# Self attention: TensorE issues the scores of heads 2 and 3 after the weighted sums instead of before them

## What is computed

```python
q, k, v = split(x @ w_qkv.T)                       # 8 batches, 16 heads, 512 tokens, 16 channels
scores = einsum('bhqd,bhkd->bhqk', q, k) * scale + bias(table)
attn = softmax(scores, axis=-1)
out = einsum('bhqk,bhkd->bhqd', attn, v).reshape(B, N, C) @ w_proj.T + b_proj
x = layernorm(x + out)
```

## Time and profile before

| | us |
|---|---|
| three timed runs | 1013.95, 1016.24, 1019.85 |
| their median | 1016.24 |
| the profiled execution | 1011.83 |
| its span, first to last instruction | 1010.0 |
| TensorE busy (weight loads 512.2) | 922.5 |
| ACT busy | 745.1 |
| DVE busy | 701.5 |
| GpSimd busy | 295.2 |

### The profile page before, as it was taken

The page is one execution under the profiler, slowest core; times in us unless marked ns, Lnnn a source line. Parts: engine busy times, 40 slices in busy tenths (PEclk is TensorE's granted clock), DMA queues, the critical chain, the costliest instruction groups (busy, mean ns, idle before and its releaser), DMA issues. The chain is left out here.

```text
span 1010.0 us, 17742 instructions
## 1 busy us (share of the span) xinstructions
PE 922.5 (91%) x5301; PEld 512.2 (51%) x5301; DVE 701.5 (69%) x1838; ACT 745.1 (74%) x1414; POOL 295.2 (29%) x349
## 2 busy tenths in 40 slices
PE   5699999999999999999999999996089999999992
PEld 2234444444444433334333433433089989998991
DVE  5378777887878878355676675586257887887883
ACT  1478878787878778899999999983047767766761
POOL 4042313141313111001122212314413434434443
PEclk9699999999999999999999999997589999999996
DMA  8987689969696867878877697641353533543550
GB/s 224 238 216 204 151 226 246 244 183 222 193 221 181 211 164 167 178 182 180 169 159 127 134 186 144 123 93 42 103 200 126 211 133 128 184 174 133 174 207 31
DMA packets 74845, 172.04 MB, mean 170 GB/s; under 512 B 16658, under 2 KB 36040, under 8 KB 64713
## 3 DMA queue, kind: packets, MB, share of 16 engines
q1 hardware_dynamic: 67944, 156.36, 61.7%
q0 software_dynamic: 6496, 14.16, 4.0%
q10 hardware_dynamic: 320, 0.52, 0.2%
HBM read 122.23 MB, written 53.73 MB: 174 GB/s over the span
## 5 line engine op out<-in xcount | busy, mean ns | idle before, releaser
L780 ACT ACTIVATE probs<-sc 128x512 f32<-128x512 f32 x1024 | 530.3, 609 | 107.7 <-DVE sc L873 81.4
L510 PE MATMUL sc<-qst,kst 57*128 57x512 f32 (+1 forms) x1024 | 258.6, 468 | 11.8 <-DMA qst<-s_qk 9.7
L873 DVE TENSOR_TENSOR sc<-sc,strip 128x308 f32<-128x308 f32 (+1 forms) x512 | 192.3, 430 | 94.2 <-PE sc L510 93.0
L522 PE MATMUL ot<-probs,vals 128*32 128x512 f32 x1600 | 214.0, 607 | 0.2 <-issue 0.2
L510 PEld LDWEIGHTS sc<-qst,kst 57*128 57x128 f32 (+1 forms) x1024 | 117.4, 185 | 162.8 <-ACT probs L780 118.6
L1757 ACT ACTIVATE f_h<-f_h_ps,par 128x384 f32<-128x384 f32 x104 | 60.9, 586 | 31.9 <-PE f_h_ps L1667 31.9
L1834 DVE TENSOR_TENSOR f_h_lo<-f_h,f_h_hi 128x384 fp32r<-128x384 f32 x104 | 65.2, 627 | 13.7 <-DVE f_h_hi L1832 5.7
L1915 POOL DMA_INDIRECT home<-s_x,get_ids x45 | 51.6, 1146 | 76.1 <-issue 43.1
L879 DVE STREAM_TRANSPOSE turned<-ot 128x512 f32<-128x512 f32 x50 | 35.4, 708 | 49.4 <-PE ot L522 45.1
L1832 DVE CAST f_h_hi<-f_h 128x384 fp32r<-128x384 f32 x104 | 37.1, 356 | 41.5 <-ACT f_h L1757 41.3
L1928 POOL DMA_INDIRECT out<-f_normed,f_put_ids x39 | 43.0, 1103 | 64.6 <-ACT f_normed L1791 56.2
(11 more groups left out here) (189 smaller groups left out, 1615.3 us busy)
## 6 DMA issues: line engine op xcount, KB each, us to landing
s_qk<-w_hi SPq DMA_DIRECT2D x32, 512.0 KB, 7.4
strip<-in_w_all SPq DMA_DIRECT2D x16, 1024.0 KB, 7.8
f_raw<-in_w_all SPq DMA_DIRECT2D x14, 1024.0 KB, 6.5
s_x<-x SPq DMA_DIRECT2D x8, 1026.0 KB, 12.1
kst<-s_qk SPq DMA_DIRECT2D x32, 256.0 KB, 6.2
qst<-s_qk SPq DMA_DIRECT2D x32, 256.0 KB, 7.4
s_x_parts<-split SPq DMA_DIRECT2D x16, 512.0 KB, 3.1
kst<-s_ctx_parts SPq DMA_DIRECT2D x32, 256.0 KB, 6.3
```

The lines of the kernel that those rows point to most:

```text
L510: nc.tensor.matmul(sc[j][:], kst[at:at + rows, i, P * c:P * c + P], qst[at:at + rows, i, :], start=True, stop=True).then_inc(scored, 1)
L522: last = nc.tensor.matmul(sums_bank(n, g)[32 * j:32 * j + 32, :], vals[:, c, 4 * g + j, :], probs[:, k % KEPT, j, :], start=(c == 0), stop ...
L780: nc.scalar.activation(probs[:, k % KEPT, j, :], sc[j][:], ACT.Exp, scale=scale).then_inc(exped, 1)
L873: nc.vector.tensor_tensor(sc[j][:, lo:hi], sc[j][:, lo:hi], band_backwards(rank_of(4 * g + j), at, hi - lo), ALU.add).then_inc(biased, 1)
```

## The change

In the self attention `scores` is called twice in a block, for heads 0 and 1 before the weighted sums and for heads 2 and 3 behind them and ahead of the side work. The wait for `ld_pair` goes with the first call. The cross attention calls it for all four heads at once, as before.

```diff
@@ tensor_program
-            def scores(n, k):
+            def scores(n, k, heads):
                 g, c = divmod(k, NC)
                 rows = FAR_ROW if n >= B and not exact else ROWS
-                if k in (0, BLOCKS // 2):
+                if k in (0, BLOCKS // 2) and 0 in heads:
                     pe.wait_ge(ld_pair[g // 2], PAIR_LOADS * (n + 1))
-                for j in range(4):
+                for j in heads:
                     at, i = spot(4 * g + j)
@@ self_body
                 for k in range(BLOCKS):
-                    scores(b, k)
+                    scores(b, k, (0, 1))
                     weigh_behind(b, k)
+                    scores(b, k, (2, 3))
                     if b < B - 1:
                         prepare_self(b + 1, k)
@@ cross_body
                 for k in range(BLOCKS):
-                    scores(n, k)
+                    scores(n, k, range(4))
                     weigh_behind(n, k)
```

## The result

| | before | after |
|---|---|---|
| median of the timed runs (20 each), us | 1016.59 | 1021.70 |
| lowest and highest | 1011.92, 1022.53 | 1016.94, 1029.67 |
| the profiled execution (its span) | 1011.83 (1010.0) | 1022.03 (1020.2) |

The ratio of after to before is 1.0049, with a 95% interval of 1.0029 to 1.0069: some 5 us slower, where 6 us faster was forecast. The two profiled executions lie 10 us apart, because the one of before is near its fastest run and the one of after near its median.

The account below looks back on a forecast made before the run. TensorE was taken as the bound, waiting 3.8 us in each of batches 1 to 6 for ACT to empty banks. Extra phases 22.4 against waits removed 28.4 gave -6.0: 1016.2 - 6.0 = 1010.2 us, range 1004 to 1022.

Parts of the forecast that it names:

- Step 1, the price of a phase: Extra score phase in 112 self attention blocks: 0.20 us each, 22.4 us cost in all (0 to 38).
- dearer phase: Rival: changing matmul shape empties the array, so an extra phase costs 0.27 us; 1018 us, chance 0.12.
- Step 2, the waits for banks: Batches 1 to 6: TensorE's waits for ACT to empty score banks go, net -3.3 us over six batches.
- list of signs: Signs of right or wrong; here, in batch 3 score loads wait for ACT under 1 us, not 5.1.
- TensorE waits in none: Tight blocks 15 to 0 and 1, and 2 to 4: banks free 0.24 and 0.29 us early, no wait.
- Step 2, the DMA at block 8: Load of the second pair at block 8 is late next; 0.2 us left for it per batch.
- signs of being wrong: Phases of 0.5 us or more, heads 0, 1 waiting for ACT, DMA wait over 0.5 at block 8, new low clock.
- Step 3, batch 7: Batch 7: shorter pause at block 4, blocks 8 to 15 at 2.2 to 2.3 us; -2.3 us (0 to -4).
- Step 4: Batch 0: extra phases against waits that go and blocks without side work; net -0.4 us (+1 to -1.5).
- The cross attention as before: Cross attention: same instructions, only starting earlier, so its length stays unchanged.
- DVE takes the place of the banks: Rival: DVE's late work behind heads 2, 3 delays the next block's bands; 1025.5 us, chance 0.17.
- The stalls only move: Rival: ACT's rhythm leaves 0.3 us waits in two or three blocks a batch; 1013.5 us, chance 0.20.

Follow-up runs that it names:

- turn_early: Changed kernel with DVE's transposition of the sums moved ahead of the bands of heads 2 and 3 (blocks 1, 5, 9, 13); 1012.18 us, ratio to before 0.9965.
- again: The same changed kernel timed and profiled once more, nothing altered; 1019.76 us, ratio to before 1.0023.
- turn_early_again: turn_early timed and profiled once more, nothing altered; 1014.75 us, ratio to before 0.9969.
- turn_early_13: Changed kernel with DVE's transposition ahead of the bands of heads 2 and 3 in block 13 alone; 1018.40 us, ratio to before 1.0037.
- turn_weights_early: turn_early with GpSimd's split of the projection weights moved ahead of its wait for the remaining loads; 1012.79 us, ratio to before 0.9954.
- whole_at_reads: Changed kernel with all four scores ahead of the sums again in blocks 2, 6, 10 and 14; 1021.57 us, ratio to before 1.0052.
- split_no_side: Changed kernel with scores split only in blocks without side work, the old order in the others; 1021.55 us, ratio to before 1.0030.
- before_turn_early: Kernel before the change with DVE's transposition moved ahead of the bands of heads 2 and 3; 1037.34 us, ratio to before 1.0178.

## Why the prediction was wrong, point by point

**Step 1, the price of a phase: right.** Two heads between sums and side work take 0.43 us, as one head had the earlier trace rows, and what follows the pair doesn't matter. The rival "dearer phase" is out. The estimate of 0.28 us a phase, worked out from the Trainium skill's TensorE: Matmul & The Clock Gate, came out too high: the rows have 2 x 0.43 - 0.66 = 0.20. The drain at a change of mode that the Trainium skill states (TensorEngine Tiling (Array Packing), Key Properties) agrees in kind, in that two heads take 0.43 instead of half of 0.66.

**Step 2, the waits for banks: they go, as worked out.** Here a row needs care. In batch 3 of after the waits read

```profile
PEld sc L510 <- ACT probs L781: 12.3, 18, 0.8
```

where the earlier trace rows had 5.1 and the forecast said under 1. The number rose, though no score phase of this batch is long for a bank: thirteen of the 18 waits are the 0.84 us that stands in front of whatever follows the sums (in the earlier trace rows the same 0.84 stands in front of the side work, as "issue"), and the others are 0.17 to 0.36 us; ACT merely finished something in that time. The phases are the measure, as the prediction itself had said of this row, and then forgot in its list of signs.

**Step 2, the sentence that failed:** "TensorE waits in none". I had checked each bank of the scores and each wait of the side work, and of the sums only their place. Their wait for DVE's transposition (`ot_read`, at blocks 2, 6, 10, 14) isn't in the working. By its own numbers it would have shown: heads 2 and 3 reach DVE at t + 1.97, their two wide bands and the transposition take some 0.7 each, so it ends at t + 3.4 at the earliest, and the sums are wanted at t + 2.76 + 0.43 = t + 3.19. DVE's "work behind them t + 2.6 to 3.3" was held against the next bands, not against the next sums. The term was sized at 0 and measured 1.0 us a batch (1.3 in batch 1), of which turn_early gives back 0.74 net in batches 2 to 6 (46.67 - 45.93). With it, batches 1 to 6 would have been forecast at -3.3 + 6.3 = +3.0 us, or +1.8 without the DMA wait; they measured +2.2.

**Step 2, the DMA at block 8:** forecast 0.2 us. By the phases it is nothing in most batches (the side work of block 7 takes 1.06 us, as in blocks 4 to 6), 0.6 in batch 5 of after, which is the 47.3 of the table, and 0.5 and 0.3 in batches 3 and 4 of turn_early. Right in kind. The forecast's own terms now add up to the measured batch: 42.4 + 3.2 + 1.0 = 46.6 us, where 46.67 was measured. Two of the signs of being wrong came in after, this wait of over 0.5 us and a half clock in batch 0, and neither is what failed.

**Step 3, batch 7: half right.** The half clock behind block 3 is gone, and block 4 takes 3.40 us instead of 5.80. But three profiles of the new order give 45.74, 43.59 and 46.37, on average 45.2, where two of the old order give 44.3. In all three the same transposition holds the sums of block 14, and longer. The loads, DVE's row and the stretch, of after:

```profile
403.78 0.18 PEld L510 LDWEIGHTS sc<-qst,kst 57*128 57x128 f32 x1 [0.30 <-ACT probs L781]
405.19 0.23 PEld L522 LDWEIGHTS ot<-probs,vals 128*32 128x32 f32 x8 [1.23 <-issue]
...
407.09 0.29 PEld L510 LDWEIGHTS sc<-qst,kst 57*128 57x128 f32 x2 [1.66 <-ACT probs L781]
```

```profile
404.42 0.70 DVE L880 STREAM_TRANSPOSE turned<-ot 128x512 f32<-128x512 f32 x1
```

```profile
404.76:411.59 6.83, 6.37 (x26) 1.86 (x26) 3.15 (x9) 4.23 (x8) 0.00 (x0) 0.50 0.22 73
```

TensorE stands until the transposition's end at 405.12, and its clock is at the lower level until the batch ends, so that the sums take 407.09 - 405.19 = 1.90 us instead of 1.00. The pause alone does not bring the half clock. In again it is just as long, and the clock stays up for the rest of the batch:

```profile
402.40 0.19 PEld L522 LDWEIGHTS ot<-probs,vals 128*32 128x32 f32 x8 [1.22 <-issue]
...
402.40:404.44 2.04, 2.01 (x14) 0.79 (x14) 1.31 (x5) 1.14 (x3) 0.00 (x0) 1.00 0.51 173
```

There the half clock comes in the first blocks of the cross attention, from 408.6 to 412.0. The three profiles of the new order and the two of the old have 3.4 or 6.8 us of it each, so the new order moved it from block 4 to the end. In turn_early, turn_early_again and turn_early_13 there is none in either place. Blocks 8 to 13 take 2.44 us each on average, where 2.2 to 2.3 was forecast and before has 2.33. With the early transposition they take 2.33 too, so no gain from two heads at a time shows in them. Batch 7 is then 42.21 and 41.65, the forecast's 41.6, but 44.63 in turn_weights_early, where block 8 starts 2.3 us late, after the DMA of its second pair, and 3.4 us of half clock follow.

**Step 4:** whether batch 0 gained its 0.4 us can't be told, since it scatters by some us. **"The cross attention as before"** failed as well: its first batch takes 38.3 to 39.0 us instead of 37.6. The loads of after at the seam:

```profile
411.44 0.35 PEld L510 LDWEIGHTS sc<-qst,kst 57*128 57x128 f32 x4 [1.66 <-ACT probs L781]
413.11 0.18 PEld L510 LDWEIGHTS sc<-qst,kst 48*128 48x128 f32 x1 [1.32 <-ACT probs L781]
413.60 0.18 PEld L510 LDWEIGHTS sc<-qst,kst 48*128 48x128 f32 x1 [0.30 <-ACT probs L781]
414.03 0.16 PEld L522 LDWEIGHTS ot<-probs,vals 128*32 128x32 f32 x8 [0.25 <-ACT probs L781]
```

The first block of the cross attention asks for all four banks at once, behind a block of the new order whose heads 2 and 3 came late: from 411.60 to the sums at 414.03 it is 2.43 us. In before it is 1.72. It is what whole_at_reads shows inside a batch, but most of it goes with the half clock just ahead: in again, where the last blocks of batch 7 ran at the full clock, the same phase takes 1.83 us, and its 38.99 has the half clock named above inside it.

**The sum.** Of the +5.1 us timed (1021.70 - 1016.59; by the interval 2.9 to 7.0), the profiles hold 2.2 in batches 1 to 6 (0.8 + 5 x 0.27, without batch 5's transfer), 0.9 in batch 7 and 1.0 at the seam, the last from the mean of three profiles, 38.6: 4.1 us. The 2.2 repeat in every profile; the 0.9 and the 1.0 are differences of means over profiles that differ among themselves by up to 2.8 and 0.7 us. The rest is inside the interval, and no stretch that repeats holds it. In batches 1 to 6 the transposition's wait is shown, by taking it away whole and in part. In batch 7 its removal at block 14 (turn_early_13) took the pause away, and no half clock came; but again had the pause and kept the clock there, so what brings the half clock stays open.

**The rivals.** "DVE takes the place of the banks" had the right engine and the right reason, late work behind heads 2 and 3, but looked for the loss at the next bands and at ACT, and priced it at 0.7 us in three places. It came at the next sums, 0.16 to 0.50 us in three places: the mechanism had a shorter way to TensorE than the one I followed. "The stalls only move" has its share as well, in the 0.2 us at block 14 of turn_early.

## What to carry to other kernels

When phases of one engine change places, write down for each phase that now starts earlier every semaphore it waits for, also those of the phases that nobody means to touch, and hold its producer's place in its own queue against the new time. A wait that is removed may have covered another; look at what ended just before it. And where two hand-written orders feed each other, move them together: here TensorE's new order cost 0.2 to 0.5%, DVE's 1.8%, and both together gained 0.3%.

## What the runs showed of the hardware that I had not expected

- A DVE multiplication (128x256, f32, the "division") that starts while GpSimd is in a subtraction over 128x1536 ends only after it. It took 3.61 us in after, and 1.80, 3.57, 3.30, 3.12 and 3.15 in before, turn_early, turn_early_13, split_no_side and before_turn_early, and in all six it ended 0.27 to 0.28 us after the subtraction. Started 0.14 us ahead of the subtraction it took its usual 0.42.
- Stretches without a weight load on TensorE of 1.23 us in batch 7 and 1.84 in batch 0 went along with stretches at half clock, 6.8 and 3.4 us long, but one of 1.22 us at the same place in again did not. The waits of 0.16 to 0.50 us in batches 1 to 6 did not either (granted clock 1.00). A wait of 4.30 us in block 0 of batch 1 went with a mean clock of 0.97 over that batch.
